# A graph-attention and mixture-of-experts kernel: the last four of sixteen message tiles summed from a high and a low part, and the experts' first weights read from memory

## The reference

```python
h = einsum('ni,hid->nhd', layernorm(x), W)            # 4 heads of 64
e = (h[src]*a_src).sum(-1) + (h[dst]*a_dst).sum(-1); e = where(e > 0, e, 0.2*e)
alpha = exp(minimum(e - segment_max(e, dst)[dst], 20.0))
alpha_norm = alpha / (segment_sum(alpha, dst)[dst] + 1e-8)
out_h = segment_sum(alpha_norm[:, :, None] * h[src], dst)
x = x + out_h.reshape(N, 256) @ W_out
t = layernorm(x)
probs = softmax(t @ router_w.T); rw, re = top_k(probs, 2); rw = rw / rw.sum(-1)
y = t
for e in range(8):
    y = y + combine[:, e:e+1] * (gelu(t @ w1[e] + b1[e]) @ w2[e] + b2[e])
x = x + y
```

## Time and profile before

| | us |
|---|---|
| median of three runs | 1675.15 |
| lowest, highest | 1672.99, 1679.77 |
| the profiled execution | 1671.1 |
| its span | 1669.0 |
| TensorE busy | 1363.9 |
| VectorE busy | 1109.7 |
| ScalarE busy | 990.6 |
| GpSimd busy | 843.7 |

### The profile page before, as it was taken

The page is one execution under the profiler, slowest core; times in us unless marked ns, Lnnn a source line. Parts: engine busy times, 40 slices in busy tenths (PEclk is TensorE's granted clock), DMA queues, the critical chain, the costliest instruction groups (busy, mean ns, idle before and its releaser), DMA issues.

```text
span 1669.0 us, 27017 instructions
## 1 busy us (share of the span) xinstructions
PE 1363.9 (82%) x7177; PEld 1120.5 (67%) x7177; DVE 1109.7 (66%) x3062; ACT 990.6 (59%) x2522; POOL 843.7 (51%) x886
## 2 busy tenths in 40 slices
PE   5731557688988888988888888888889898989998
PEld 4530335477777777777777777777777776777887
DVE  6522656576777677777777777777777777777643
ACT  3530545465666666666666666666666676767733
POOL 1237556555556555656555555555555555553000
PEclk9875776689999999999999999999999999999999
DMA  9354454333333333434333334343434343456000
GB/s 221 95 166 126 108 158 116 102 100 99 108 102 113 100 110 104 113 101 113 101 109 104 108 96 119 96 119 99 111 100 118 100 114 96 118 92 96 1 17 16
DMA packets 89806, 174.66 MB, mean 105 GB/s; under 512 B 22471, under 2 KB 56081, under 8 KB 89625
## 3 DMA queue, kind: packets, MB, share of 16 engines
q0 software_dynamic: 40448, 111.89, 26.3%
q1 hardware_dynamic: 48103, 60.78, 12.3%
q10 hardware_dynamic: 1106, 0.27, 0.1%
HBM read 159.26 MB, written 14.43 MB: 104 GB/s over the span
## 4 chain that ended last, share of the span: by engine, by line
PE 39%; DVE 23%; issue 14%; another core or an unknown queue 10%; ACT 6%; ACTq 1%; DVEq 1%
PE agg_ps L1162 12%; PE ob L1235 11%; PE hb L1189 8%; DVE ring L863 7%; DVE y L1000 4%; ACT acc L1396 2%; PE ob L1271 2%; DVE oh L798 2%; ACT agg_ps L1399 1%; PE ob L1241 1%; PE kbank L1130 1%; DVE dsum L803 1%; PE ob L1311 1%; DVE stat L918 1%
## 5 line engine op out<-in xcount | busy, mean ns | idle before, releaser
L753 POOL DMA_INDIRECT ring<-table,srcE x832 | 811.7, 976 | 611.0 <-PE agg_ps L1162 330.7
L1162 PE MATMUL agg_ps<-ring,oh 128*128 128x260 f32 x1664 | 543.5, 425 | 30.1 <-ACT agg_ps L1399 13.6
L1396 ACT COPY acc<-agg_ps x831 | 307.7, 370 | 353.7 <-PE agg_ps L1162 126.3
L1235 PE MATMUL ob<-w_sb,hT 128*125 128x256 f32 x1600 | 417.0, 386 | 37.8 <-DVE y L1000 34.2
L1235 PEld LDWEIGHTS ob<-w_sb,hT 128*125 128x125 f32 x1600 | 296.9, 190 | 100.7 <-issue 33.3
L1162 PEld LDWEIGHTS agg_ps<-ring,oh 128*128 128x128 f32 x1664 | 307.8, 207 | 83.2 <-issue 27.5
L1399 ACT COPY agg_ps<-zc 128x260 f32 x832 | 314.6, 378 | 28.6 <-issue 2.3
L863 DVE TENSOR_TENSOR ring<-ring,kbank 128x1024 f32<-128x1024 f32 x208 | 244.7, 1214 | 48.5 <-ACT ring L1418 28.2
L1000 DVE SCALAR_TENSOR_TENSOR y<-ob,cmb,y 125x256 f32<-125x256 f32 x400 | 189.2, 476 | 100.7 <-PE ob L1235 62.2
L1428 ACT ACTIVATE hT<-hb,b_sb 128x375 f32<-128x375 f32 (+1 forms) x272 | 153.9, 566 | 137.8 <-PE hb L1189 86.1
L798 DVE TENSOR_TENSOR oh<-kbank,relE 128x512 f32<-128x512 f32 x208 | 141.8, 682 | 137.8 <-remote 105.0
(11 more groups left out here) (285 smaller groups left out, 1416.8 us busy)
## 6 DMA issues: line engine op xcount, KB each, us to landing
OT<-relb_d SPq DMA_DIRECT2D x52, 512.0 KB
ring<-table,srcE POOLq DMA_INDIRECT x832
y<-in_x_dram SPq DMA_DIRECT2D x50, 125.0 KB
out_dram<-y SPq DMA_DIRECT2D x50, 125.0 KB
table<-hrow SPq DMA_DIRECT2D x25, 227.5 KB
acc<-in_x_dram SPq DMA_DIRECT2D x2, 1568.0 KB
acc<-in_L_ffn_w_dram SPq DMA_DIRECT2D x1, 2048.0 KB
w_sb<-in_L_ffn_w_dram SPq DMA_DIRECT2D x1, 2048.0 KB
```

Of the source, the lines that this page charges most:

```text
L753: pool.indirect_dma_start(out=rings[b % RING][:, k, :], out_offset=None, in_=table[:, :], in_offset=bass.IndirectOffsetOnAxis(ap=srcE[:, t ...
L1162: T.matmul(bank_of[k // 8][k % 8], oh[:, (4 * b + q) % OHQ, k % 4, :], rings[b % RING][:, k, :], start=False, stop=True, skip_group_check= ...
L1235: t = T.matmul(o[0:Q, 0:D], hT[:, e % 2, f, cols], w2_sb[:, e, f, :], start=f == 0, stop=f == KC - 1)
L1396: A.copy(row_of[h][k % 8], closed[h][k % 8]).then_inc(S["ev"], 1)
```

## The change

- The fourth quad of each batch is summed from two parts. ScalarE copies its messages, rounded to fp32r, into `high` (`high_parts`, step 3 of the iteration that sums the batch); VectorE subtracts these from the messages into `low`, in two halves of two tiles (`low_parts`, behind `across` at step 5 and behind `whole` at step 7). `aggregate` multiplies `low` and `high` by a one-hot matrix in fp32r, two matmuls for a tile.
- The comparison of that quad goes from step 2, ahead of `front`, to step 6. TensorE's product at step 7 waits for it now.
- The room for this in SBUF comes from w1. Its parts are made in `w1x`, three slots deep, between steps 8 and 23 of the start, stored to `w1_d`, and from then on each expert's 512 KB are loaded again in each group, by SyncE, 14 steps ahead of their first use.
- The two comparisons of `combine` that depend on the router's choice alone (L978, L979) go to `differences`. `begin_y` (L988) goes from the end of a group's preparation to step 1 of its experts, which on VectorE stands behind `front`.

```diff
-        w1h, w1l = (sb(n, [P, NE, KC, D], F32R) for n in ("w1h", "w1l"))
+        RW = 3
+        w1x = sb("w1x", [P, RW, 2, KC, D], F32R)
...
+            HIGH_AT, LOW_AT = {3: 3}, {5: (3, 0), 7: (3, 1)}
+            SPLIT1 = {BT // 2 + 2 * e: e for e in range(NE)}
+            LOAD1 = {BT * START + 6 * n - 20: n for n in range(NE * GROUPS)}
...
+                    def load_w1(n):
+                        r, e = n % RW, n % NE
...
+                        if n >= RW:
+                            sp.wait_ge(S["h1"], 2 * (n - RW + 1))
+                        sp.dma_start(w1x[:, r].rearrange("p s k n -> p (s k n)").bitcast(F32), w1_d[e * P:(e + 1) * P, :]).then_inc(w1_ld[r], 16)
...
+                    def low_parts(b, q):
+                        j, t = q[0] - SQ, 2 * q[1]
+                        dve.wait_ge(S["mh"], (QUADS - SQ) * b + j + 1)
+                        v.tensor_tensor(low[:, j, t:t + 2], rings[b % RING][:, 4 * q[0] + t:4 * q[0] + t + 2, :], high[:, j, t:t + 2],
+                                        ALU.subtract).then_inc(S["ml"], 1)
...
-                        if k == 2 and 0 <= it < NBAT:
-                            if b < NBAT:
-                                dve.wait_ge(S["D"], b + 1)
+                        steps(it, k)
+                        if 0 <= it < NBAT and k in LOW_AT:
+                            low_parts(it, LOW_AT[k])
...
+                        if k == 6 and 0 <= it < NBAT:
                             onehot(it, 3)
...
                         elif k == 7:
-                            pe.wait_ge(S["CC"], b + 1)
+                            if b > 0:
+                                pe.wait_ge(S["oh"], QUADS * b + 1)
...
-                        T.matmul(bank_of[k // 8][k % 8], oh[:, (4 * b + q) % OHQ, k % 4, :], rings[b % RING][:, k, :],
-                                 start=False, stop=True, skip_group_check=True).then_inc(S["agg"], 1)
...
+                            T.matmul(bank_, ohr[:, j, k % 4, :], low[:, j, k % 4, :], start=False, stop=False, skip_group_check=True)
+                            T.matmul(bank_, ohr[:, j, k % 4, :], high[:, j, k % 4, :], start=False, stop=True, skip_group_check=True).then_inc(S["agg"], 1)
...
+                        if f == 0:
+                            pe.wait_ge(w1_ld[r], 16 * ((NE * g + e) // RW + 1))
...
+                    def high_parts(b, q):
+                        j = q - SQ
+                        act.wait_ge(S["msg"], QUADS * b + q + 1)
+                        if b > 0:
+                            act.wait_ge(S["agg"], BT * (b - 1) + 4 * q + 4)
+                        A.copy(high[:, j], rings[b % RING][:, 4 * q:4 * q + 4, :]).then_inc(S["mh"], 1)
```

More of the change, by code:

```diff
@@ L68, in gnn_ffn_kernel @@
     tab_d = internal("tab_d", (5, GT), I32)
+    w1_d = internal("w1_d", (NE * P, 2 * KC * D))
     with ExitStack() as ctx:
@@ L595, in gnn_ffn_kernel @@
             ring4 = [a[:, :, :].rearrange("p k (h w) -> p k h w", h=H) for a in rings]
-            oh = s2("oh", [P, OHQ, 4, P])
+            SQ = 3
+            oh = s2("oh", [P, SQ, 4, P])
+            ohr = s2("ohr", [P, QUADS - SQ, 4, P], F32R)
+            high, low = (s2(n, [P, QUADS - SQ, 4, ROW], F32R) for n in ("high", "low"))
             OT = s2("OT", [P, BT * P], BF16)
@@ L654, in gnn_ffn_kernel @@
             ld_w1, ld_ffn, ld_b2 = sem("ld_w1"), sem("ld_ffn"), sem("ld_b2")
+            w1_st = [sem(f"w1_st{r}") for r in range(RW)]
+            w1_ld = [sem(f"w1_ld{r}") for r in range(RW)]
             fld = [sem(f"fld{r}") for r in range(RING)]
@@ L718, in store_y, with store_w1 @@
                             sp.dma_start(out[bass.ds(rows_[i], Q), :], y[0:Q, u, i, :]).then_inc(y_st[u], 16)
+                    def store_w1(e):
+                        sp.wait_ge(S["w1l"], e + 1)
+                        sp.dma_start(w1_d[e * P:(e + 1) * P, :], w1x[:, e % RW].rearrange("p s k n -> p (s k n)").bitcast(F32)).then_inc(w1_st[e % RW], 16)
+                    def load_w1(n):
+                        r, e = n % RW, n % NE
+                        if n == 0:
+                            for q in range(RW):
+                                sp.wait_ge(w1_st[q], 16 * len(range(q, NE, RW)))
+                        if n >= RW:
+                            sp.wait_ge(S["h1"], 2 * (n - RW + 1))
+                        sp.dma_start(w1x[:, r].rearrange("p s k n -> p (s k n)").bitcast(F32), w1_d[e * P:(e + 1) * P, :]).then_inc(w1_ld[r], 16)
                     fetch(0)
@@ L739, in _ @@
                                 load_x(p + 1)
+                        for sl in range(it * BT, (it + 1) * BT):
+                            if sl - 1 in SPLIT1:
+                                store_w1(SPLIT1[sl - 1])
+                            if sl in LOAD1:
+                                load_w1(LOAD1[sl])
                     store_y(GROUPS - 1)
@@ L1078, in blocks @@
                     def blocks(it, k):
-                        if it == 1 and k < NE:
-                            low_w1(k)
+                        if it * BT + k in SPLIT1:
+                            low_w1(SPLIT1[it * BT + k])
                         elif it == 2 and k == 5:
@@ L1084, in blocks @@
                         if p is not None and 0 <= p < GROUPS:
+                            if s0 + k == 1:
+                                begin_y(p)
                             experts(p, s0 + k)
@@ L1091, in blocks @@
                                 combine(p + 1)
-                                begin_y(p + 1)
                     for it in range(-1, LAST):
@@ L1199, in hidden @@
                             pe.wait_ge(S["gl"], HC(g, e, f) - 2)
+                        r = (NE * g + e) % RW
+                        if f == 0:
+                            pe.wait_ge(w1_ld[r], 16 * ((NE * g + e) // RW + 1))
                         fs = slice(f * P, (f + 1) * P)
-                        exact(hbank[f][:, 0:w], [(w1h[:, e, k, fs], w1l[:, e, k, fs]) for k in range(KC)],
+                        exact(hbank[f][:, 0:w], [(w1x[:, r, 0, k, fs], w1x[:, r, 1, k, fs]) for k in range(KC)],
                               [(xTh[:, u, k, 0:w], xTl[:, u, k, 0:w]) for k in range(KC)]).then_inc(S["h1"], 1)
@@ L1458, in high_w1 @@
                         act.wait_ge(ld_w1, 16)
-                        A.copy(w1h[:, e, :, :], w1raw[:, e, :, :]).then_inc(S["w1c"], 1)
+                        if e >= RW:
+                            act.wait_ge(w1_st[e % RW], 16 * (e // RW))
+                        A.copy(w1x[:, e % RW, 0], w1raw[:, e, :, :]).then_inc(S["w1c"], 1)
                     def weights(g):
@@ L1478, in _ @@
                                 evacuate(it, k)
-                            if it == 0 and k >= BT - NE:
-                                high_w1(k - BT + NE)
+                            if it * BT + k in SPLIT1:
+                                high_w1(SPLIT1[it * BT + k])
                             elif it == NBAT and k == 0:
                                 evacuate_last()
+                            if k in HIGH_AT:
+                                b = it + 1 if k == 15 else it
+                                if 0 <= b < NBAT:
+                                    high_parts(b, HIGH_AT[k])
                             if k == 9 and it + 1 < NBAT and p is not None:
```

30 lines of the change are left out of this document (21 added, 9 removed).

## The result

The changed kernel takes 1693.1 us in the median (four runs, 1689.0 to 1694.7) against 1674.1: a ratio of 1.0108, with a 95% interval of 1.0071 to 1.0145. It is slower by 1.1%. The forecast was 1671 us and no change; the time lies in the range (1638 to 1702) but on the wrong side of the 0.5% bound. The profiled execution has a span of 1687.2 us against 1669.0, 18.2 more.

A forecast was written before the change was run, and what follows sets the result against it. The loop was taken as bound by TensorE's work at some points, VectorE's at others. 15 groups x (0 + 0.1 - 0.4) = -4.5, early +6, late -5: -3.5 us on the 1675.15 median, rounded to 1671; range 1638 to 1702.

The forecast's parts named there:

- VectorE's and ScalarE's added time: Two subtraction halves add 1.22 us a batch, 63 in all; ScalarE's copy 1.05 us, 55 in all, taken as hidden.
- TensorE's saving: Fp32r sums in steps 12 to 15 save 0.19 us a tile, 0.77 a batch, 40 us of work in all.
- rival 1: TensorE's work decides: VectorE's additions fit its gaps and 27 of the 40 us saved come, 1648 us; chance 0.35.
- Second batch: Second batch of a group: 0.61 us gained at step 3, 0.61 given back by the second half before `y`; sum 0.
- Third batch: Third batch of a group: L1140 comes 0.77 us later, mostly recovered by shorter `combine` and steps 12 to 15; sum +0.1.
- First batch: First batch of a group: 0.61 us gained at step 3, given back by step 5, 0.3 saving kept; sum -0.4.
- Late groups: From group 11 on, waits for `eC` are long, so the 0.61 us is kept in some 8 batches: -5 us.
- Early batches: Seven batches before the experts, bound by the chain alone, each lose 0.85 us after the gain at step 3: +6.
- w1: Loading 71 MB of w1 again raises the DMA share from 0.40 to 0.58 and costs 0, hidden by 14 steps' lead.
- rival 3: Loads of w1 lengthen fetches or register loads by 0.5 us a batch, 26 us in all: 1701 us; chance 0.09.
- The narrow range: The sum's own range, 1660 to 1684 us, described as 1 us more or less in each kind of batch.
- Rival 2: Slower at step 7, where TensorE's product waits for a half of `low` and a comparison: 1695 us; chance 0.18.

The follow-up runs named there:

- e6: Changed kernel, `high` and `low` still made and awaited, but the fourth quad summed in one plain fp32 matmul as before: 1498.46 us, ratio 1.0265.
- e5: Changed kernel with ScalarE's copy and VectorE's two subtractions made in the first batch alone: ratio 1.0004 to the kernel before.
- e2: Changed kernel with `begin_y` and the router's two comparisons back in their old places: ratio 1.0225 to the kernel before.
- e16: Changed kernel with both halves of the subtraction moved to steps 9 and 10: ratio 1.0038 to the kernel before, which took 1675 us beside it.
- c0: The kernel before, run unchanged in the 1460 us runs: ratio 1.0003.
- c1: The changed kernel, run unchanged in the 1460 us runs: 1494.25 us, ratio 1.0228 to the kernel before.
- e1: Changed kernel with each load of w1 moving 8 of its 1024 columns only: ratio 1.0209 to the kernel before.

## Why the prediction was wrong

The step that failed is the overlap: the half, the comparison and the second half were taken to fit into VectorE's idle time, so that a group came to -0.3 us (0 for the second batch, +0.1 for the third, -0.4 for the first). Measured were +0.91 in the traces of the result and +2.21 in the 1460 us runs. With it failed the -5 of the late groups. By kinds and terms:

- **VectorE's and ScalarE's added time** was right for one instruction: 682 ns a half (677 read from the nearest row), 1.05 us for the copy (1.05), and 0.61 from a half to the next start. In total it came out lower, 58 and 48 us for 70 and 55.
- **TensorE's saving** was mis-sized: 0.12 to 0.145 us a tile, not 0.19, because a row from an all-fp32r stretch was used for tiles between plain products. TensorE's busy time fell by 23 us in the 1460 us runs. Of what is saved, e6 shows 4 us in the time. That rival 1 would bring 27 was out of reach.
- **Second batch**: "the half (0.61) and the comparison (0.61) fill the 1.26 us for which VectorE was idle", and the second half gives 0.61 back at `y`: "Sum 0". In the result's traces it is -0.04, with a standard error of 0.4 after the change; in the 1460 us runs it is +1.24, of which 1.1 is the wait for `y`, forecast as +0.6. e5 shows that the copy and the halves are what costs here (1.19).
- **Third batch**: the waits were right, about 1 us at step 7 (1.04 measured) and L1140 0.77 later (0.65 of wait at step 9). The sum of +0.1 fits the +0.21 of the 1460 us runs; the -0.22 of the result's traces is too uncertain to count.
- **First batch**: "the half and the comparison fit ahead of TensorE's step 7, and the saving at the end is kept in part, 0.3. Sum -0.4". It was +1.17 in the result's traces, and +0.76 in the 1460 us runs. The first clause nearly holds: the wait at step 7 is 0.05 us there and at most 0.55 in the result's trace. The saving is what did not stay: TensorE then waits for ScalarE's clearing of a bank (0.57 us, 0.44 even in e5, which has no copies) and for `y`. Of the +0.76 only 0.1 (means) to 0.3 (medians) go back to the copy and the halves; `begin_y` is worth 0.19 (e2), given back in the third batch. In the result's trace TensorE waits in first batches mostly for L1533 of ScalarE (1.48 us a batch, 0.02 before). e16, which has hardly any loss, shows the same 28.42 us as the result. So what makes the +1.17 stays open.
- **Late groups**: -5 was forecast from a wait of 2.46 for `eC`, kept in full. In place of it a group became 1.6 us longer. The gain at step 3 was real (60.4 for 76.6 us over the span) and was spent at steps 7 and 9, in these groups as in the others.
- **Early batches**: +6 forecast, +6.9 measured in one pair of traces, but +1.0 between c0 and c1. The agreement may be luck. In the first pair the granted clock between 200 and 300 us also fell from 0.69 to 0.59, with TensorE busy for 63.7 in place of 67.2 us, which the forecast did not have; between c0 and c1 it did not fall in this window (0.73 and 0.74).
- **w1**: right at 0, and rival 3 wrong. In the window above, a DMA share of 0.53 stands for the 0.58 estimated. The Trainium skill's page "DMA: Bandwidth & Descriptors" (Latency and other measured facts) has a latency of 2 us at high load; no lengthening of a batch with load shows between c1 and e1, at 177 and 124 GB/s. No run here measures that latency itself.
- **The narrow range**: 1660 to 1684 was said to be 1 us more or less in each kind of batch. 15 groups of three batches would be 45 us either way.

The room was also read from a trace that flatters it. From the end of `across` to `argument` VectorE is idle for 0.7, 1.6 and 1.3 us in a third, first and second batch of the kernel before (means of ten groups, trace), but for 0.28, 0.55 and 0.38 in c0. The additions are 1.83 us a batch, and with them 0.2 to 0.3 us are left in both kinds of trace. That goes with a loss of 1.1% in the one and 2.3% in the other; no run separates this from the rest of the difference.

Rival 2, with a chance of 0.18, comes nearest: its 1695 us against 1693.1, and the order of VectorE's instructions as the cause. But its mark, waits of over 1 us at step 7 in all three kinds, did not appear: they are 1.04, 0.05 and 0.19. So its number came near partly by luck; much of the loss is at `y`. I had taken the second batch's 1.26 us of idle VectorE as room for the half; idle time ahead of an instruction that waits for TensorE is no room when the addition stands ahead of what TensorE waits for.

## What to carry to other kernels

Between two engines that answer each other in turns, an added instruction has a place on the chain and a place beside it, one instruction apart: first what releases the other engine, then the filler. Count savings on an engine only up to its next wait, and take the price of a product from rows with the same neighbours before and behind. Where a change has several parts, the cheapest one alone may be the gain: here the comparison's move without the split, 0.3 to 0.5% in the sets in which it ran.

## What was not expected of the hardware

The same kernel takes 1460 us in two sets of runs and 1643 to 1675 in the others, up to 15% apart, at a granted clock of 0.952 and 0.926 in the profiled runs of c0 and of the kernel before. Since the chip number 9 stands with both times, whether the chip or something else makes this difference is open. The longer runs have waits that the profile can put down to nothing on the core. The largest of VectorE's and ScalarE's in the kernel before, in the trace:

```profile
DVE oh L798 <- remote: 105.0, 32, 25.1
DVE y L1000 <- remote: 29.5, 11, 3.3
```

```profile
ACT acc L1396 <- remote: 98.6, 25, 30.5
ACT hT L1428 <- remote: 36.6, 11, 4.2
```

The trace of c0 has none of this kind on any engine. In the middle a group takes 83.87 us in the one and 72.74 in the other, 3.7 us a batch. Of these 11.1 us of a group 8.2 are idle time of TensorE (10.0 against 1.85), in stops of up to 3.5 us in which several engines stand still. Their cause stays open. They matter for the reading: they give VectorE free time (the 2.20 us of the earlier trace rows). The added work cost 1.1% where they are and 2.3% where they are not.
